# Image mixing network in the frequency domain: the first row pair's inverse along w starts inside the inverse along h, GpSimd's tail is reordered, and the filter output's write order is turned

## The reference, cut to what matters

```python
h = layer_norm(x, n1_g, n1_b)
xf = rfft2(h, axes=(1, 2))                  # along h and w, for each channel
o1 = relu(complex 16 x 16 block product of xf with w1, plus b1)
o2 = complex 16 x 16 block product of o1 with w2, plus b2
yf = softshrink(real(o2), 0.01) + 1j * softshrink(imag(o2), 0.01)
h = irfft2(yf) + h + x
out = gelu(layer_norm(h, n2_g, n2_b) @ mw1 + mb1) @ mw2 + mb2 + h
```

## Time and profile before

| | |
|---|---|
| three executions, median | 1784.01 us |
| the profiled execution | 1787.48 us, of which the span from first to last instruction is 1785.7 us |
| busy: PE, DVE, ACT, POOL | 1636.1, 1195.5, 934.6, 630.5 us |
| mean granted TensorE clock | 0.977 of full speed |
| `filter_` in step 1 | 546.5 to 649.2 us |
| `idft_h` in step 1 | 649.2 to 679.0 us |
| `mlp` in step 1 | 679.0 to 934.8 us |

### The profile page before, as it was taken

The page is one execution under the profiler, slowest core; times in us unless marked ns, Lnnn a source line. Parts: engine busy times, 40 slices in busy tenths (PEclk is TensorE's granted clock), DMA queues, the critical chain, the costliest instruction groups (busy, mean ns, idle before and its releaser), DMA issues.

```text
span 1785.7 us, 35087 instructions
## 1 busy us (share of the span) xinstructions
PE 1636.1 (92%) x11184; PEld 1453.6 (81%) x11184; DVE 1195.5 (67%) x2880; ACT 934.6 (52%) x1778; POOL 630.5 (35%) x756
## 2 busy tenths in 40 slices
PE   0099989999999998999999998999999999899999
PEld 0088878888889887888889887888888988688888
DVE  7959956666646976666664895666664697566663
ACT  4335426666634534666652452666663453466665
POOL 4800004777750001677781000477775000111111
PEclk9999989999998998999998999999999999999999
DMA  8210061333320033333330006133332003211111
GB/s 246 100 54 1 1 220 59 101 105 105 100 80 1 1 115 117 103 103 106 106 101 24 1 1 220 54 97 103 106 107 84 1 1 126 77 36 31 34 36 48
DMA packets 164896, 138.85 MB, mean 78 GB/s; under 512 B 9186, under 2 KB 127332, under 8 KB 164804
## 3 DMA queue, kind: packets, MB, share of 16 engines
q1 hardware_dynamic: 164516, 137.15, 24.0%
q10 hardware_dynamic: 288, 0.46, 0.1%
HBM read 70.47 MB, written 67.11 MB: 77 GB/s over the span
## 4 chain that ended last, share of the span: by engine, by line
PE 44%; DVE 21%; POOL 17%; issue 15%; ACT 1%; DVEq 1%; DMA 1%; SPq 0%; POOLq 0%; ACTq 0%
PE ps L641 13%; PE ps L496 7%; PE ps L590 6%; POOL arena L1191 6%; POOL gz L1160 4%; DVE vsb L942 4%; POOL gz L1164 4%; PE ps L632 4%; PE ps L634 3%; PE ps L633 3%; DVE csb L944 3%; DVE usb L931 3%; DVE usb L932 2%; POOL arena L1198 2%; PE ps L621 2%
## 5 line engine op out<-in xcount | busy, mean ns | idle before, releaser
L641 PEld LDWEIGHTS ps<-mw,gel 128*128 128x128 f32 x4096 | 533.2, 191 | 43.3
L641 PE MATMUL ps<-mw,gel 128*128 128x128 f32 x4096 | 536.4, 274 | 0.0
L751 ACT ACTIVATE gel<-ps,mb1f 128x512 f32<-128x512 f32 x512 | 351.6, 687 | 269.9 <-PE ps L634 238.7
L1198 POOL TENSOR_TENSOR arena<-arena,mb2rep 128x512 f32<-128x512 f32 x128 | 163.5, 1277 | 886.0 <-ACT hn L737 886.0
L632 PE MATMUL ps<-hth,mw1h 128*128 128x512 f32 x512 | 262.9, 513 | 8.1 <-DVE htl L1024 7.8
L1191 POOL TENSOR_SCALAR arena<-xnext,rstd,shift 128x128 f32<-128x128 f32 x384 | 168.4, 457 | 217.7 <-DVE shift L1127 217.7
L737 ACT ACTIVATE hn<-arena,shift,rstd 128x128 f32 (+1 forms) x512 | 221.6, 482 | 35.6 <-DVE shift L1127 35.6
L1007 DVE TENSOR_TENSOR arena<-ps,arena 128x512 f32 (+1 forms) x64 | 44.2, 691 | 266.0 <-PE ps L613 241.9
L496 PE MATMUL ps<-cst,arena 128*128 128x128 f32 x1024 | 130.2, 294 | 90.3 <-DVE arena L904 81.4
L634 PE MATMUL ps<-hth,mw1l 128*128 128x512 f32 x512 | 204.4, 399 | 0.0
L496 PEld LDWEIGHTS ps<-cst,arena 128*128 128x128 f32 x1024 | 129.4, 208 | 90.8 <-DVE arena L904 81.5
(11 more groups left out here) (92 smaller groups left out, 2428.8 us busy)
## 6 DMA issues: line engine op xcount, KB each, us to landing
arena<-aside SPq DMA_DIRECT2D x128, 256.0 KB, 5.0
aside<-gz SPq DMA_DIRECT2D x96, 256.0 KB, 3.0
between<-xout SPq DMA_DIRECT2D x62, 256.0 KB, 2.3
xnext<-between SPq DMA_DIRECT2D x62, 256.0 KB, 3.0
out_dram<-xout SPq DMA_DIRECT2D x62, 256.0 KB, 2.3
aside<-first SPq DMA_DIRECT2D x32, 256.0 KB, 2.0
xnext<-in_x_dram SPq DMA_DIRECT2D x31, 256.0 KB, 3.0
mw1raw<-in_L_mw_dram SPq DMA_DIRECT2D x4, 256.0 KB, 2.5
```

Of the source, the lines that this page charges most:

```text
L641: mm = pe.matmul(ps[:, r % 2, P * i:P * i + P], gel[:, r % 2, m, P * i:P * i + P], mw2[:, m, :], start=(m == 0 and i == 0), stop=(m == CHU ...
L751: act.activation(gel[:, r % 2, m, :], ps[:, 2 + m % 2], ACT.Gelu, bias=mb1f[:, m:m + 1]).then_inc(gelu_out, 1)
L1198: pool.tensor_tensor(t, t, b, ALU.add).then_inc(mb2_done, 1)
```

## The change

Three things are changed.

1. `mlp`'s first pair. The products for the columns that come from the first 24 of 32 channel groups (`SOON = 24`) are issued inside `idft_h`, after group 25; the last quarter is issued where the whole first pair stood. DVE adds them to the residual in two portions: the first (`h2_soon(s, 0, SOON)`) between its last four copies, the second in pair 0. `split_weights` and the wait for the first residual tiles move from pair 0 to this place as well.
2. The tail of `mlp` when another step follows. POOL computes all four last tiles' rows before it does their `scale` and `residual`. DVE does `x_new` of tile 29 after the sums of tiles 30 and 31, no longer before.
3. `shrink`'s last subtraction runs over channels outside and frequency parts inside (eight adjacent values written, inputs read in steps of 64 values) where it ran over frequency parts outside and channels inside (inputs read in order, each value written 128 values after the last).

```diff
+SOON = 24
@@ block.tensor
+            def first_pair(s, a, b):
+                if a == 0:
+                    pe.wait_ge(h2_done, TILES * s)
+                for v in (v_act, v_dve):
+                    pe.wait_ge(v, CGROUPS // 2 * s + b // 2)
+                t = slice(GROUP // 2 * a, GROUP // 2 * b)
+                for bank, m, h0 in ((6, DE, 0), (7, DO, H - ROWS)):
+                    dst = ps[:, bank, ROWS * GROUP * a:ROWS * GROUP * b]
+                    mm = pe.matmul(dst, m, v_of(s)[:, t, h0:h0 + ROWS, :], start=(a == 0), stop=True,
+                                   skip_group_check=True)
+                mm.then_inc(iw_soon if a == 0 else iw_mm, 1)
@@ def idft_h(s)
                     mm.then_inc(ih_mm, 1)
+                    if cg == SOON + 1:
+                        first_pair(s, 0, SOON)
@@ def mlp(s)
-                pe.wait_ge(h2_done, TILES * s)
-                for half in range(2):
...
-                mm.then_inc(iw_mm, 1)
+                first_pair(s, SOON, CGROUPS)
@@ block.vector, shrink
-                dst = dst.rearrange("p c k -> p k c")
-                v, cl = (t.rearrange("p j r c -> p (j r) c") for t in (v, cl))
+                v, cl = (t.rearrange("p j r c -> p c (j r)") for t in (v, cl))
                 dve.tensor_tensor(dst, v, cl, ALU.subtract).then_inc(y_done, 1)
@@
+            def h2_soon(s, a, b):
+                t = slice(GROUP // 2 * a, GROUP // 2 * b)
...
+                own.add(dve.tensor_tensor(top, even, top, ALU.add))
+                yield
+                own.add(dve.tensor_tensor(low, even[:, ::-1], low, ALU.add))
+                yield
+                own.settle()
+                own.add(dve.tensor_tensor(top, odd[:, ::-1], top, ALU.add))
+                ins = dve.tensor_tensor(low, low, odd, ALU.subtract)
...
@@ the step's loop on DVE
-                with dve.Fori(0, CGROUPS // 4) as j:
+                with dve.Fori(0, SOON // 4) as j:
                     for r in (1, 3):
                         v_out_(s, 4 * j + r, r)
+                split_weights(s)
+                dve.wait_ge(resid_in[0], RESID_IN[0] * (s + 1))
+                v_out_(s, SOON + 1, 1)
+                dve.wait_ge(iw_soon, s + 1)
+                sums = h2_soon(s, 0, SOON)
+                next(sums)
+                v_out_(s, SOON + 3, 3)
+                next(sums)
+                v_out_(s, SOON + 5, 1)
+                next(sums)
+                v_out_(s, SOON + 7, 3)
@@ def pair(i, h)
-                    if known >= 3:
+                    if 3 <= known <= PAIRS or last and known > PAIRS:
                         x_new(s, i + (2 * h - 5) // 4, (2 * h - 5) % 4)
...
+                    if known > PAIRS and not last:
+                        x_new(s, i + (2 * h - 5) // 4, (2 * h - 5) % 4)
@@ block.gpsimd, after tile 31 of the loop
+                j = TILES // 4 - 1
+                if not last:
+                    ready(j, 0)
+                    z_rows(j, 0)
+                    z_rows(j, 1)
+                for n in (TILES - 2, TILES - 1):
+                    biased(n)
+                if not last:
+                    ready(j, 2)
+                    z_rows(j, 2)
+                    z_rows(j, 3)
+                    scaled(j, 0)
+                    for r in range(4):
+                        if r < 3:
+                            scaled(j, r + 1)
+                        added(j, r)
```

More of the change, by code:

```diff
@@ L997, in shift_bias @@
                 dve.tensor_tensor(mb1f[:, :], ps[:, 5, 0:CHUNKS], mb1[:, :], ALU.add).then_inc(mlp_b, 1)
+            def h2_soon(s, a, b):
+                t = slice(GROUP // 2 * a, GROUP // 2 * b)
+                top, low = (by_row(resid_of(s)[:, ROWS * e:ROWS * e + ROWS, :])[:, :, t] for e in range(2))
+                even = ps[:, 6].rearrange("p (t h e) -> p h t e", h=ROWS, e=2)[:, :, t]
+                odd = ps[:, 7].rearrange("p (t h e) -> p h t e", h=ROWS, e=2)[:, :, t]
+                own.add(dve.tensor_tensor(top, even, top, ALU.add))
[5 more added lines that the diff above has]
+                ins = dve.tensor_tensor(low, low, odd, ALU.subtract)
+                if b == CGROUPS:
+                    ins.then_inc(h2_done, 2)
+                else:
+                    own.add(ins)
+                yield
             def h2(s, i, h):
@@ L1198, in bias @@
                     pool.tensor_tensor(t, t, b, ALU.add).then_inc(mb2_done, 1)
-                def tile(j, r):
-                    n = 4 * j + r
-                    known = n if isinstance(j, int) else 8
-                    nxt = not last
-                    m = n - 4
-                    again = nxt and known >= 4
-                    if again:
-                        h0 = ROWS * tile_of(j - 1, r)
-                        pool.wait_ge(rs_done, RS * s + 2 * j + r // 2 + 1)
-                        z_rows(j - 1, r)
-                        pool.wait_ge(z_new, TILES * s + m + 1)
-                        if s or m >= 4:
-                            pool.wait_ge(gz_st[r], 16 * (TILES // 4 * s + j - 1))
-                        scale(s + 1, h0, gz[:, r])
-                    if 2 <= known <= TILES + 1:
-                        pool.wait_ge(hn_done, TILES * s + n - 1)
-                        bias(s, j + (r - 2) // 4, (r - 2) % 4)
-                    if again:
-                        pool.wait_ge(gz_done, R_POOL0 + TILES * s + m + 1)
-                        residual(gz[:, r], xnext[:, r], gz[:, r])
@@ L1221, in _, with ready, scaled @@
-                for n in range(TILES + 4):
-                    tile(n // 4, n % 4)
+                def ready(j, r):
+                    pool.wait_ge(rs_done, RS * s + 2 * (j + 1) + r // 2 + 1)
+                def scaled(j, r):
+                    m = 4 * j + r
+                    pool.wait_ge(z_new, TILES * s + m + 1)
+                    if s or m >= 4:
+                        pool.wait_ge(gz_st[r], 16 * (TILES // 4 * s + j))
+                    scale(s + 1, ROWS * tile_of(j, r), gz[:, r])
@@ new lines, in added, with biased @@
+                def added(j, r):
+                    pool.wait_ge(gz_done, R_POOL0 + TILES * s + 4 * j + r + 1)
+                    residual(gz[:, r], xnext[:, r], gz[:, r])
+                def biased(n):
+                    pool.wait_ge(hn_done, TILES * s + n + 1)
+                    bias(s, n // 4, n % 4)
+                for n in range(TILES):
+                    j, r = n // 4 - 1, n % 4
+                    if j >= 0 and not last:
+                        ready(j, r)
+                        z_rows(j, r)
+                        scaled(j, r)
+                    if n >= 2:
+                        biased(n - 2)
+                    if j >= 0 and not last:
+                        added(j, r)
```

18 lines of the change are left out of this document (8 added, 10 removed).

## The result

The changed kernel takes 1818.22 us (1817.73 to 1825.06, 4 runs) where the kernel before, measured beside it, takes 1787.06 us (1781.05 to 1790.13, 4 runs): 1.019 of the time, interval 1.0164 to 1.0216. So it is slower by 31 us by the medians and by 34 us by the ratio. The forecast of 1777 us was wrong in sign, and the range up to 1790 did not hold it. The profiled execution took 1818.51 us (span 1816.7).

A forecast was written before the change was run, and what follows sets the result against it. DVE was taken to bound the filter, TensorE `idft_h` and most of `mlp`. Terms -5.4, -6.2, +4.5 and 0 sum to -7.1 us: profiled 1787.48 to 1780.4, 1777 us by the median; range 1752 to 1790.

The forecast's parts named there:

- part 3: `shrink`'s subtraction in the filter, new write order: price stays 1.06 us, so 0 us over 128 operations.
- the high bound: Filter subtraction: each of two hopping inputs pays what the scattered writes pay, +0.37 us an operation.
- this rival: Filter subtraction: two hopping inputs each pay, 1.43 us an operation, +46 us, 1823 us; chance 0.08.
- comes 1:1 into the stage: Filter: DVE sets the pace, so any change in its subtraction's cost passes fully into the stage.
- The rival of 1731 us: Filter subtraction: reads hop for nothing and ACT and TensorE have room, so 46 us go as well; chance 0.12.
- Part 1: `idft_h` to `lower` in `mlp`'s first pair: -1.35 us a step, -5.4 us over four steps.
- the insertion: `idft_h`, ahead of the last copy: four added records of 384 columns cost 1.35 us, counted in full.
- Part 2, steps 0 to 1 and 2 to 3: `mlp` tail into `dft_w`: the 4.43 us wait goes, a later one comes; -3.1 us twice, -6.2 us.
- The successor: `dft_w`: `put_aside` delays the store of tile 29, so TensorE stands 3 us after four groups.
- the two cases: `dft_w` behind the new wait: clock falls, stage ends at 545.2 (-1.3), or holds, 541.6 (-4.9).
- Part 2, steps 1 to 2: `mlp` tail, building of block matrices: DVE's operations stretched beside POOL's products, +4.5 us, bounds 0 and +6.

The follow-up runs named there:

- e11: The changed kernel with 72 words in place of 64 between neighbouring rows of both arrays the subtraction reads: 1795.25 us, ratio 1.0069.
- e4: The kernel before with the layout turned in the bias addition, which reads PSUM with hops, so the subtraction reads in order: 1764.18 us, ratio 0.9883.
- The probe: A separate kernel, no part of the network: DVE alone does the 512-value subtraction in thirteen forms, six times each; all in order takes 692 ns.
- e5: The kernel before with only the change to `mlp`'s first pair: 1779.86 us, ratio 0.9957.
- e1: The changed kernel with the old write order of the subtraction: 1782.23 us, ratio 0.9989 of the kernel before.
- e6: The kernel before with only the change to the tail of `mlp`: 1786.62 us, ratio 0.9991.
- e7: e1 with SP's last four stores issued ahead of the four put_asides: 1767.74 us, ratio 0.9881 of the kernel before.
- e8: e7 with the 24 operations building the block matrices moved before pair 14 of step 1's `mlp`: 1772.56 us, ratio 0.9921 of the kernel before.
- e10: e7 with e4's layout, the building spread over step 1's first `mlp` pairs and `last_tile` before the remaining preparation: 1740.81 us, ratio 0.9757 of the kernel before.
- e12: e10 with the rest of the new layer's preparation moved behind DVE's eighth copy in `dft_w`: 1737.0 us, ratio 0.9727 of the kernel before.
- e2: The kernel before with only the new write order of the subtraction: 1822.56 us, ratio 1.021.

## Why the prediction was wrong

**The failed step is the price in part 3:** "I take its price, 1.06 us: 0 us over 128 operations". The choice was made by resemblance (as many hops, on the other side), and it counted the two hopping streams as one. Measured, one stream that hops by 256 bytes or more costs 0.33 us for 512 values, on either input or on the output in SBUF (1.02 against 0.69), a second one on the inputs 0.22 more (1.24). In the kernel that is 1.29 against 1.06. The prediction had both ends: it said the high bound was each input paying for itself, 1.43 us, gave it 0.08, and worked out that it decides from 1.19 us on. The measured value lies past that point, some two thirds of the way from the taken price to the rival's (0.235 of 0.37). The mechanism of this rival is right, and its chance of 0.08 was far too small, since nothing in the rows spoke against it. Of the 0.37 us that it added, a third did not come; that its 1823 us lies within 5 us of the measured 1818 is partly luck, as the unit grew by more than the operation.

**The cost per operation wasn't all.** 29.2 us are the subtraction's own; the unit grew by 0.30 us and not by 0.235. The next operation, which used to start 0.16 us before the subtraction's end, now starts 0.09 us before it (medians; the rows are with e11), so DVE's time from one start to the next grew by 0.29 us: 37.5 us for 128 units. DVE's other operations also show some 6 us more busy time over the program (1.7 for L950, 1.9 for L939 and 2.2 for L940, 422 ns against the 405 of L932, 128 times each), most of it inside such overlaps: from start to start they grew by 0.02 us a unit. The prediction's "what DVE's subtraction costs more or less comes 1:1 into the stage" is right in that DVE sets the pace of a slower filter; but the operation's own time is not what it costs.

**DVE does not set the pace of a faster filter.** "ACT (1.5 us a unit) and TensorE have room" is false for TensorE: in e4 the subtraction became 0.37 us shorter, and the unit 0.19, since TensorE's work for a unit is 2.66 us. The rival of 1731 us counted on 46 us, about twice what was to be had; e4 gave 21. The prediction had the hint before it, TensorE busy for 99.45 of 102.70 us in the earlier trace rows, and set it aside.

**The price of a hopping stream.** The prediction cited the Trainium skill, Vector Engine (DVE) Microarchitecture Reference, section 5.2, for 1.71 ns a column with a hopping destination and up to 1.76 with hopping sources. The probe agrees for one source or the destination: (1018 - 143) / 512 = 1.71 and (1023 - 143) / 512 = 1.72. With both sources hopping by 256 to 4096 bytes (and the output in runs of eight, which alone cost nothing) it is (1246 - 143) / 512 = 2.15 and not 1.76; only at 288 bytes is it near the page, (1075 - 143) / 512 = 1.82. The measurement decides. The prediction's sum did not rest on it.

**Part 1** was put at -1.35 us a step. The way from the last copy to the first sums was to shrink by 0.45 + 1.64 = 2.1 us, against 1.35 us for the insertion; the earlier trace rows have 682.86 - 678.86 = 4.0 us before, and the changed kernel:

```profile
695.27 0.69 DVE L365 COPY arena<-ps 128x512 f32<-128x512 f32 x1 [0.17 <-PE ps L605]
...
697.87 1.43 DVE L887 BATCH_NORM_STATS2 stats<-arena 128x6 f32<-128x256 f32 x4
701.55 0.17 DVE L1169 SCALAR_TENSOR_TENSOR shift<-stats,rstd 128x8 f32<-128x8 f32 x1
...
705.00 0.69 DVE L1050 TENSOR_TENSOR htl<-ps,hth 128x512 fp32r<-128x512 f32 x1 [0.70 <-ACT hth L753]
```

has 697.87 - 695.96 = 1.9 us (the long additions now stand between copies). The way from the shift to `lower` is 3.45 us against 3.25 forecast and 3.86 before. -2.1 - 0.4 + 1.35 for the insertion is -1.15, and e5's row of the table gives -1.0 a step: mechanism right, forecast a little too large.

**Part 2, steps 0 to 1 and 2 to 3** was put at -3.1 each. Measured -1.6 and -2.2 in the changed kernel, -3.2 and -2.5 in e1 and -0.8 and -1.2 in e6, which have the same passages; one profile doesn't tell the size better. The successor is there as named: the wait before the first product is gone, TensorE stands 3.38 us before the fifth group where 3 was forecast, and the store left 2.8 us after `mlp`'s last product (521.65 against 514.22 + 4.63 = 518.85; forecast 512.3 against 509.62). e7 shows the cause: with the store ahead, the wait is gone and 30.0 us remain. The clock was low behind the wait (0.54), the worse of the two cases between which the prediction took the middle.

**Part 2, steps 1 to 2** was put at +4.5: measured +4.2 (+5.2 in e1), by the mechanism named, L870 going on only in part beside POOL's products (16 in 10.48 us). What the prediction did not name is that the operation on `betarow`, which stands behind these, is held there for 8 us once they are out of the way; it kept this passage at 40.5 us in e8 and at 37.6 in e10, where e12 has 30.7.

**Sum.** Parts 1 and 2 forecast -7.1 us, e1 gave -2 (-4.5 to +0.5). Part 3 forecast 0, e2 gave +37. Together they make 35, against the 34 measured.

## What to carry

Count the streams that hop, not the hops of one, and ask which side pays nothing: here an input in PSUM could turn the layout for free, while the SBUF inputs of the next operation could not. Take the price of an operation from start to start where the next one can begin before it has ended. Price a gain by the engine that comes next, too: its own work per unit is the floor. And in a queue that one engine issues in order, put the transfer that a buffer waits for ahead of the one that nobody does; e7 is one added line, and 15 to 19 us.

## What was not expected of the hardware

- Two inputs of DVE from SBUF that both hop cost 1.24 us for 512 values and one alone 1.02; the pair costs only 1.075 us with steps of 288 bytes. The probe doesn't tell why 256, 512 and 4096 are alike and 288 isn't.
- The first input in PSUM hops by 256 bytes for nothing: 691 ns against 692.
- The operation behind the subtraction is shown starting 0.16 us before its end when the output hops, and 0.09 us before it when the inputs do (medians of 116 units). No run shows why.
- A destination with steps of 96 bytes is dearer than one with steps of 512: 1435 against 1023 ns.
- An operation of DVE on 128 values, all in SBUF, took 7.98 us beside POOL's two-input products and 0.20 us beside none, while copies from PSUM took 0.69 us in either (e12). The Trainium skill, SBUF — State Buffer, section Who interferes with whom, has it that DVE and GpSimd share a second pair of ports as an exclusive lock, which `tensor_scalar` in its faster modes and operations with two SBUF inputs need. The rows agree, and they show more: this operation of DVE was not held for one of POOL's operations but until a whole run of them was over: the rest of one and six more, up to 919.63; and as long in e8 (8.03 us). The building operations with two inputs in SBUF did get in between: seven in 7.5 us beside the products of the changed kernel.
